# Feed-forward of an AdaLN block on one Trainium2 core: the gate-up groups of a step in one piece, the down products behind them

## The chip, the cores and the metric

One NeuronCore of a Trainium2 chip runs the whole program. The metric is the time of one execution on the device in microseconds (us), the median of three runs. TensorE (PE, with its weight loads as PEld), VectorE (DVE), ScalarE (ACT) and GpSimd (POOL) each work through their own list of instructions in order and wait for each other through semaphores. TensorE's matmul products go to eight PSUM banks of 128 x 512 float32; ScalarE and VectorE read them from there.

## The reference, cut to what matters

```python
h = _layernorm(x) * (1 + ca) + sa            # x is [1, 4096, 512]
x = x + ga * attn(h)                         # mixer: qkv, cumulative sums, SwiGLU
h = _layernorm(x) * (1 + cb) + sb
# feed-forward; weights are 4-bit values with a scale for each 128 inputs
gate_up = einsum('bsh,oh->bso', h, w_gu)     # 512 -> 2 * 1408
gate, up = gate_up[..., :1408], gate_up[..., 1408:]
hid = silu(gate) * up
y = einsum('bsi,hi->bsh', hid, w_down)       # 1408 -> 512
y = y / sqrt(mean(y * y) + 1e-6)
return x + gb * y
```

## The kernel before, in words

The program has two stages one behind the other: `mixer` (until about 1357 us of the span) and `ffn` (from there on). The change touches `ffn` alone.

`ffn` takes the 4096 tokens in NB = 8 blocks of T = 512. In a block it goes through I_T = 11 steps j, one for each 128 of the 1408 hidden units. A step has GROUPS = 8 gate-up groups m: m = 0 to 3 are the gate, one group for each 128 of the 512 inputs (they have scales of their own, so they can't be summed in PSUM), and m = 4 to 7 are the up part. A group is two matmuls (line 1856: the high and the low half of the activations) into one of the evacuation banks. Banks 0 to 3 serve in turn (`ev_bank`: m % 4). Bank 3 is also R, which takes the column sums for the norm, so in some steps (`r_steps`: step 5 of each block, steps 4 to 7 of block 0) the groups turn over banks 0 to 2 alone.

The groups are taken out of PSUM in pairs. ScalarE takes an even group (`take`, line 1926: copy with scale), then VectorE takes the odd one and adds the even (`take`, line 2119: multiply, add). GpSimd adds the two pair sums of the gate and of the up part (`half`, line 2008). ScalarE applies silu (line 1936), VectorE multiplies the two (`hidden`, line 2126), ScalarE rounds to the float16 part HH high (`high`, line 1932), GpSimd subtracts for the low part (`low`, line 2025). Each of these is one step late in its engine's order: behind the group-3 take of step j stands `hidden(j - 1)` on VectorE, ahead of the group-6 take `high(j - 1)` on ScalarE, and GpSimd does, in a step, half 0 of j, `low(j - 1)`, then half 1 of j.

The down product of a step is 4 output chunks c with 3 matmuls each (`down`, line 1820: high weights by high HH, low by high, high by low), 12 in all, summed over the 11 steps in banks 4 to 7. TensorE does it two steps late: in step j it does `down(b, j - 2, c)`. Only c = 0 waits for HH (both parts). For the first step of a block each c also waits for that chunk's bank to be copied out (`copy_y`, line 1894).

`before(j, m, steps)` gives the group that used a bank last; TensorE waits until that one is taken out before it starts group m.

Beside this, the previous block is finished at fixed places (place = 4 * j + m // 2, four in a step): ScalarE copies y out at places 8 to 11 (step 2), squares it at 12, 13, 14, 16 (line 1888); GpSimd adds the squares at 15, 16, 19 (line 2016); TensorE sums over partitions at 22 (`y_square`, line 1806, step 5, before m = 4), ScalarE keeps the sum (line 1908) and takes the root at 23 (line 1912, with an activation table load ahead of it and ahead of the next silu); VectorE takes groups 4 and 6 of that step in ScalarE's place (`open_tile`, line 2110), inverts at 24, 26, 27, 28 (line 2075) and multiplies, `norm_y` (line 2094), at 29, 32, 33, 36, each ahead of the odd take of its place; GpSimd adds the residual (`result`, line 2021) at 31, 35, 39, 43. Block 0 has, instead of this, the layer norm of the mixer's last block (lines 2065 to 2099 on VectorE, 1882 to 1916 on ScalarE, 1995 to 2003 on GpSimd).

A tile `A[slot]` of the taken groups and `HH[slot]` have two slots that alternate (the last step of a block has a third): the first take of step j waits for `low(j - 2)` (`slot_free`).

Of the kernel before, what the change touches and what calls it, by code (L numbers as in the profile page):

```python
# [1606 lines left out]
def ffn(nc, v):  # L1607


    T, NB, DT, I_T, GU, D = v["T"], v["NB"], v["DT"], v["I_T"], v["GU"], v["D"]  # L1610
# [4 lines left out]
    with ExitStack() as ctx:  # L1615
# [27 lines left out]
        def slot(j):  # L1643


            return 2 if j == I_T - 1 else j % 2
# [4 lines left out]
        def r_steps(b):  # L1651

            return range(4, 8) if first(b) else range(5, 6)

        def ev_bank(j, m, steps):
            return (GROUPS * (j - steps.start) + m + 1) % 3 if j in steps else m % 4

        def before(j, m, steps):

            for back, last in ((0, m), (1, GROUPS)):  # L1660
                same = [k for k in range(last) if ev_bank((j - back) % I_T, k, steps) == ev_bank(j, m, steps)]
                if same:
                    return back, same[-1]
            assert ev_bank(j, m, steps) == 3
            return None
# [25 lines left out]
        def first(b):  # L1691
            return isinstance(b, int) and b == 0
# [26 lines left out]
        def opened(b, j, m):  # L1719

            if by_vector(b, j, m):
                return opened_dve, len(OPENS) * b + opens(b).index((j, m)) + 1
            skipped = sum(1 for o in opens(b) if o < (j, m))
            return by_act, (DT * I_T - len(OPENS)) * b + DT * j + m // 2 + 1 - skipped
# [62 lines left out]
        @block.tensor  # L1787
        def _(pe):
            def sums_left(b, steps):

                pe.wait_ge(by_dve, DT * (I_T * b + steps.start))
                pe.wait_ge(*opened(b, steps.start - 1, GROUPS - 2))

            def mean():
                pe.wait_ge(x_sum, NSUM)
                nc.tensor.matmul(R[:], ones[:], RS[:], start=True, stop=True).then_inc(mean_red, 1)

            def variance():
                pe.wait_ge(sq_sum, NSUM)
                pe.wait_ge(centred, DT)  # L1800
                nc.tensor.matmul(R[:], ones[:], RS[:], start=True, stop=True).then_inc(var_red, 1)

            def y_square(b):
                pe.wait_ge(y_sum, NSUM * (b + 1))
                pe.wait_ge(*((var_kept, 1) if first(b) else (y_kept, b)))
                nc.tensor.matmul(R[:], ones[:], RSY[:], start=True, stop=True).then_inc(y_red, 1)

            def down(b, j, c):
                if c == 0:
                    if j == 0 and first(b):  # L1810
                        pe.wait_ge(down_loaded, 32)
                    pe.wait_ge(HH_high, I_T * b + j + 1)
                    pe.wait_ge(HH_low, I_T * b + j + 1)
                if j == 0 and first(b):
                    pe.wait_ge(last_ready, c + 1)
                elif j == 0:
                    pe.wait_ge(y_copied, DT * (b - 1) + c + 1)
                col = j * D + c * P
                for w, part in ((down_hi, 0), (down_lo, 0), (down_hi, 1)):
                    mm = nc.tensor.matmul(O[c][:], w[:, col:col + P], HH[:, slot(j), part, :],  # L1820
                                          start=(j == 0 and w is down_hi and part == 0),
                                          stop=(j == I_T - 1 and part == 1))
                if c == DT - 1:
                    mm.then_inc(down_used, 1)

            for b in range(NB):
                s, steps = b % 2, r_steps(b)
                if not first(b):
                    pe.wait_ge(H_loaded[s], 16 * ((b + 1) // 2))
                for j in range(I_T):  # L1830
                    for m in range(GROUPS):
                        place = DT * j + m // 2
                        if m % 2 == 0 and first(b) and place == MEAN:
                            sums_left(b, steps)
                            mean()
                        if m % 2 == 0 and first(b) and place == VARIANCE:
                            variance()
                        if m % 2 == 0 and not first(b) and place == Y_MEAN:
                            sums_left(b, steps)
                            y_square(b - 1)  # L1840
                        last = before(j, m, steps)
                        if last is None:
                            pe.wait_ge(*((var_kept, 1) if first(b) else (y_kept, b)))
                        elif not (j == 0 and last[0] and first(b)):

                            back, k = last
                            if k % 2:
                                pe.wait_ge(by_dve, DT * (I_T * b + j - back) + k // 2 + 1)
                            elif j < back:
                                pe.wait_ge(*opened(b - 1, I_T - 1, k))  # L1850
                            else:
                                pe.wait_ge(*opened(b, j - back, k))
                        which, g = m // DT, m % DT
                        col = (g * 2 * I_T + which * I_T + j) * P
                        for part in range(2):
                            mm = nc.tensor.matmul(EV[ev_bank(j, m, steps)][:], values[:, col:col + P], H[s][:, part, g, :],  # L1856
                                                  start=part == 0, stop=part == 1)
                        mm.then_inc(group_done, 1)


                        if m % 2:
                            if j >= 2:
                                down(b, j - 2, m // 2)
                            elif not first(b):
                                down(b - 1, I_T - 2 + j, m // 2)

            for j in (I_T - 2, I_T - 1):
                for c in range(DT):
                    down(NB - 1, j, c)
            pe.wait_ge(y_kept, NB - 1)  # L1870
            pe.wait_ge(by_dve, DT * I_T * NB)
            pe.wait_ge(*opened(NB - 1, I_T - 1, GROUPS - 2))
            for c in range(DT):
                pe.wait_ge(y_squared, DT * (NB - 1) + c + 1)
                mm = nc.tensor.matmul(R[:], ones[:], SQY[:, c, :], start=c == 0, stop=c == DT - 1)
            mm.then_inc(y_red, 1)
# [324 lines left out]
```

## Time and profile before

| what | before |
|---|---|
| median of 3 runs (lowest, highest) | 1942.83 us (1942.53, 1943.8) |
| the profiled execution: its time, its span | 1943.23 us, 1941.4 us |
| mean granted TensorE clock | 0.992 |
| TensorE busy over the span (matmul) | 1872.4 us, 96% |
| VectorE, ScalarE, GpSimd busy | 72%, 48%, 47% |
| stage `ffn` in the span | from 1356.95 us to the end |

The profile is of one execution. In a timeline row the first number is the start in us from the start of the span, the second the time until the last instruction of the row ended; neighbours of one kind are merged (x4), and matmul records overlap: a row of one matmul lasts 0.38 us while the next starts 0.2155 us after it. What stands in square brackets is the idle time of that engine ahead of the row, and who ended it.

### The profile page before, as it was taken

The page shows a single profiled execution, that of the slowest core. Times are in us where ns is not written, and L with a number is a line of the kernel's source. Part 1 is how long each engine was busy: PE and PEld are TensorE (multiplying, and loading weights), DVE is VectorE, ACT ScalarE, POOL GpSimd, SP SyncE. Part 2 cuts the span into 40 slices and gives each one's busy share as a digit, 9 for nine tenths or more (in the row PEclk, how much of TensorE's full clock was granted, in tenths as well). Part 3 has the DMA queues.
Part 4 walks back from the last instruction along what each step waited for, and adds up shares of the span by engine and source line. Part 5 has one row for each costly group of instructions (what it writes and reads, how often), then busy time and mean ns, then how long its engine had stood idle before and what let it go on. Part 6 is the DMA issues. An engine that isn't in the chain of part 4 may idle for free. (4 is left out here: it accounts for less than half of the span.)

```text
span 1941.4 us, 24528 instructions
## 1 busy us (share of the span) xinstructions
PE 1872.4 (96%) x8382; PEld 830.3 (43%) x8382; DVE 1399.3 (72%) x1787; ACT 924.8 (48%) x1414; POOL 909.7 (47%) x644
## 2 busy tenths in 40 slices
PE   6999999999999999999999999999999999999996
PEld 2443444444444444444444444444344444444442
DVE  6979768776867876877786686653677667767765
ACT  6753444235234434423533431221676766776673
POOL 2655435234314423422342331311768787777774
PEclk9999999999999999999999999999999999999998
DMA  8312220220202112021020121213210111011011
GB/s 309 130 55 65 76 70 24 75 66 18 81 20 70 51 40 69 11 87 60 24 74 17 48 66 33 88 39 113 118 44 22 44 66 59 8 66 66 1 44 65
DMA packets 70894, 120.44 MB, mean 62 GB/s; under 512 B 5024, under 2 KB 32672, under 8 KB 69152
## 3 DMA queue, kind: packets, MB, share of 16 engines
q1 hardware_dynamic: 70816, 119.45, 18.4%
q8 instruction: 43, 0.70, 0.1%
q14 instruction: 35, 0.29, 0.0%
HBM read 80.11 MB, written 39.32 MB: 62 GB/s over the span
## 5 line engine op out<-in xcount | busy, mean ns | idle before, releaser
L733 PE MATMUL bank<-Y,wsw 128*128 128x512 f16 x3072 | 689.9, 381 | 21.2 <-ACT late L939 14.4
L1140 POOL TENSOR_TENSOR late<-late 128x512 f16<-128x512 f32 x128 | 182.7, 1428 | 622.6 <-ACT late L947 621.9
L733 PEld LDWEIGHTS bank<-Y,wsw 128*128 128x128 f16 x3072 | 299.5, 98 | 394.6 <-ACT late L939 17.8
L2119 DVE SCALAR_TENSOR_TENSOR f_A<-bank,gu_s,f_A 128x512 f32<-128x512 f32 x352 | 259.9, 742 | 163.7 <-ACT f_A L1926 156.9
L708 PE MATMUL bank<-late,wout 128*128 128x512 f16 x1536 | 352.4, 379 | 0.4 <-POOL late L1140 0.4
L2008 POOL TENSOR_TENSOR f_A<-f_A 128x512 f32<-128x512 f32 x176 | 261.6, 1488 | 126.1 <-DVE f_A L2119 126.1
L1926 ACT ACTIVATE f_A<-bank,gu_s 128x512 f32<-128x512 f32 x336 | 229.1, 684 | 140.5 <-PE bank L1856 121.1
L1820 PE MATMUL bank<-f_HH,f_down_hi 128*128 128x512 f16 x704 | 266.8, 381 | 11.5 <-POOL f_HH L2025 11.2
L1206 DVE TENSOR_TENSOR late<-late,bank 128x512 f32<-128x512 f32 x128 | 87.3, 682 | 201.8 <-PE bank L733 192.7
L708 PEld LDWEIGHTS bank<-late,wout 128*128 128x128 f16 x1536 | 150.2, 98 | 188.8 <-issue 12.7
L939 ACT ACTIVATE late<-bank 128x512 f32<-128x512 f32 x128 | 76.4, 597 | 323.0 <-PE bank L733 279.4
L655 PE MATMUL bank<-H,wqkv 128*128 128x512 f16 x1008 | 225.8, 382 | 4.2 <-ACT H L800 4.2
L947 ACT ACTIVATE late<-late 128x512 f16<-128x512 f32 x128 | 80.4, 628 | 265.2 <-DVE late L1206 265.2
L1856 PE MATMUL bank<-H,wqkv 128*128 128x512 f16 x704 | 181.6, 379 | 2.9 <-DVE f_A L2119 1.9
L1856 PE MATMUL bank<-f_H,wqkv 128*128 128x512 f16 x704 | 182.2, 379 | 1.8 <-DVE f_A L2119 1.2
L655 PEld LDWEIGHTS bank<-H,wqkv 128*128 128x128 f16 x1008 | 99.1, 98 | 132.6 <-issue 20.4
L1820 PE MATMUL bank<-f_HH,f_down_lo 128*128 128x512 f16 x352 | 134.1, 381 | 0.0
L1820 PEld LDWEIGHTS bank<-f_HH,f_down_hi 128*128 128x128 f16 x704 | 69.0, 98 | 110.8 <-issue 34.5
L2025 POOL TENSOR_TENSOR f_HH<-f_A,f_HH 128x512 f16<-128x512 f32 x88 | 102.6, 1166 | 10.7 <-ACT f_HH L1932 10.6
L1322 DVE RECIPROCAL K<-K 128x512 f32<-128x512 f32 x32 | 107.0, 3344 | 0.0
L1856 PEld LDWEIGHTS bank<-H,wqkv 128*128 128x128 bf16 x704 | 67.3, 98 | 91.7 <-DVE f_A L2119 10.2
L1856 PEld LDWEIGHTS bank<-f_H,wqkv 128*128 128x128 bf16 x704 | 68.0, 98 | 88.7 <-DVE f_A L2119 6.6
(220 smaller groups left out, 2146.2 us busy)
## 6 DMA issues: line engine op xcount, KB each, us to landing
X<-xT SPq DMA_DIRECT2D x14, 1024.0 KB, 5.4
room<-packed SPq DMA_DIRECT2D x48, 176.0 KB, 2.4
h_scratch<-X SPq DMA_DIRECT2D x8, 1024.0 KB, 4.4
f_X<-x_scratch SPq DMA_DIRECT2D x8, 1024.0 KB, 5.5
x_scratch<-X SPq DMA_DIRECT2D x28, 256.0 KB, 2.2
h_scratch<-SQ SPq DMA_DIRECT2D x28, 256.0 KB, 2.2
outT<-f_X SPq DMA_DIRECT2D x7, 1024.0 KB, 4.3
room<-wswT SPq DMA_DIRECT2D x4, 1024.0 KB, 6.5
```

What stands on the lines that cost most here:

```text
L655: mm = nc.tensor.matmul(out[:], wqkv[:, pw, k, col:col + P], halves[:, px, k, :], start=(k == 0 and pw == 0 and px == 0), stop=(k == DT - ...
L708: mm = nc.tensor.matmul(O_BANK[c][:], wout[:, pw, j, c * P:(c + 1) * P], UG[:, j % 2, px, :], start=(j == 0 and pw == 0 and px == 0), stop ...
L733: mm = nc.tensor.matmul(out[:], wsw[:, pw, k, col:col + P], Y[:, px, k, :], start=(k == 0 and pw == 0 and px == 0), stop=(k == DT - 1 and ...
L1140: nc.gpsimd.tensor_tensor(UG[:, j % 2, 1, :], G, UG[:, j % 2, 0, :], ALU.subtract).then_inc(UG_low, 1)
L1206: nc.vector.tensor_tensor(dst, a, b_, ALU.mult).then_inc(done, 1)
L1322: nc.vector.reciprocal(K[:, c, :], K[:, c, :]).then_inc(inverted, 1)
L1820: mm = nc.tensor.matmul(O[c][:], w[:, col:col + P], HH[:, slot(j), part, :], start=(j == 0 and w is down_hi and part == 0), stop=(j == I_T ...
L1856: mm = nc.tensor.matmul(EV[ev_bank(j, m, steps)][:], values[:, col:col + P], H[s][:, part, g, :], start=part == 0, stop=part == 1)
L1926: nc.scalar.activation(A[:, slot(j), 2 * which + g // 2, :], EV[ev_bank(j, m, steps)][:], ACT.Copy, scale=gu_s[:, t, g:g + 1]).then_inc(by ...
L2008: nc.gpsimd.tensor_tensor(a, a, A[:, slot(j), 2 * which + 1, :], ALU.add).then_inc(halves, 1)
L2025: nc.gpsimd.tensor_tensor(HH[:, slot(j), 1, :], A[:, slot(j), 0, :], HH[:, slot(j), 0, :], ALU.subtract).then_inc(HH_low, 1)
L2119: nc.vector.scalar_tensor_tensor(a, EV[ev_bank(j, m, steps)][:], gu_s[:, which * I_T + j, g:g + 1], a, ALU.mult, ALU.add).then_inc(by_dve, 1)
```

## The change

In a step TensorE issued two groups, then the three down matmuls of chunk 0, two groups, chunk 1, and so on. Now it issues all eight groups, then the twelve down matmuls, chunk 0 to 3. Nothing else is changed: neither the instructions, nor their banks, nor the order on any other engine. The column sum of step 5 (and those of block 0 in steps 4 and 7) keeps its place between the groups.

```diff
                         mm.then_inc(group_done, 1)
 
-                        if m % 2:
-                            if j >= 2:
-                                down(b, j - 2, m // 2)
-                            elif not first(b):
-                                down(b - 1, I_T - 2 + j, m // 2)
+
+                    for c in range(DT):
+                        if j >= 2:
+                            down(b, j - 2, c)
+                        elif not first(b):
+                            down(b - 1, I_T - 2 + j, c)
 
             for j in (I_T - 2, I_T - 1):
                 for c in range(DT):
```

## Rows read from the trace of the kernel before

**Rows 1.** Windows: length, busy PE, PEld, DVE, ACT, POOL, clock, DMA, GB/s.

```profile
1357.00:1431.00 74.00, 66.70 (x294) 27.47 (x295) 54.87 (x76) 48.80 (x76) 50.67 (x37) 1.00 0.24 91
...
1602.90:1672.20 69.30, 68.38 (x312) 29.99 (x311) 48.33 (x66) 48.20 (x76) 53.84 (x41) 1.00 0.13 46
...
1920.00:1925.00 5.00, 4.32 (x12) 1.54 (x12) 0.00 (x0) 0.00 (x0) 0.54 (x1) 0.66 0.66 211
```

**Rows 2.** Timeline of TensorE: an ordinary step, the sum, two waits.

```profile
1602.88 1.03 PE L1856 MATMUL bank<-f_H,wqkv 128*128 128x512 f16 x4
...
1646.83 1.03 PE L1856 MATMUL bank<-H,wqkv 128*128 128x512 f16 x4
...
1648.34 1.03 PE L1856 MATMUL bank<-H,wqkv 128*128 128x512 f16 x4
...
1671.32 1.02 PE L1806 MATMUL bank<-f_RSY,ones 128*128 128x512 f32 x2
...
1672.17 0.59 PE L1856 MATMUL bank<-H,wqkv 128*128 128x512 f16 x2
...
1693.92 1.20 PE L1856 MATMUL bank<-H,wqkv 128*128 128x512 f16 x4
1695.84 0.38 PE L1820 MATMUL bank<-f_HH,f_down_hi 128*128 128x512 f16 x1 [0.72 <-POOL f_HH L2025]
```

**Rows 3.** Waits (total us, times, longest): 1602.9 to 1672.2; 1357 to 1431.

```profile
DVE f_A L2119 <- ACT f_A L1926: 19.3, 29, 1.4
...
ACT f_A L1926 <- POOL f_HH L2025: 5.5, 5, 1.5
```

**Rows 4.** Timeline of the first groups of block 0, without down products.

```profile
1356.95 5.50 PE L1856 MATMUL bank<-H,wqkv 128*128 128x512 f16 x24 [0.33 <-PEq L107]
...
1357.58 0.69 ACT L1926 ACTIVATE f_A<-bank,gu_s 128x512 f32<-128x512 f32 x1 [5.08 <-PE bank L1856]
...
1358.37 2.48 DVE L2119 SCALAR_TENSOR_TENSOR f_A<-bank,gu_s,f_A 128x512 f32<-128x512 f32 x3 [5.88 <-ACT f_A L1926]
...
1359.17 0.55 PEld L1856 LDWEIGHTS bank<-H,wqkv 128*128 128x128 bf16 x4 [0.40 <-DVE f_A L2119]
...
1360.04 0.55 PEld L1856 LDWEIGHTS bank<-H,wqkv 128*128 128x128 bf16 x4 [0.32 <-DVE f_A L2119]
```

**Rows 5.** Timeline of ScalarE in step 2 of block 4.

```profile
1650.08 0.59 ACT L1894 ACTIVATE f_Y<-bank 128x512 f32<-128x512 f32 x1
1650.56 0.69 ACT L1926 ACTIVATE f_A<-bank,gu_s 128x512 f32<-128x512 f32 x1
1651.13 0.61 ACT L1894 ACTIVATE f_Y<-bank 128x512 f32<-128x512 f32 x1
```

**Rows 6.** Timeline of VectorE, block 4: two `norm_y`, a take, `hidden`.

```profile
1684.36 0.74 DVE L2094 SCALAR_TENSOR_TENSOR f_Y<-f_Y,mod,f_RY 128x512 f32<-128x512 f32 x1
1685.01 0.74 DVE L2119 SCALAR_TENSOR_TENSOR f_A<-bank,gu_s,f_A 128x512 f32<-128x512 f32 x1
1685.68 0.68 DVE L2126 TENSOR_TENSOR f_A<-f_A 128x512 f32<-128x512 f32 x1
...
1695.81 1.66 DVE L2094 SCALAR_TENSOR_TENSOR f_Y<-f_Y,mod,f_RY 128x512 f32<-128x512 f32 x1
```

**Rows 7.** Timeline of GpSimd, block 4, steps 7 to 9.

```profile
1685.84 1.65 POOL L2008 TENSOR_TENSOR f_A<-f_A 128x512 f32<-128x512 f32 x1 [1.48 <-DVE f_A L2119]
1687.45 1.15 POOL L2025 TENSOR_TENSOR f_HH<-f_A,f_HH 128x512 f16<-128x512 f32 x1
1688.57 1.72 POOL L2021 TENSOR_TENSOR f_X<-f_X,f_Y 128x512 f32<-128x512 f32 x1
...
1695.65 1.27 POOL L2021 TENSOR_TENSOR f_X<-f_X,f_Y 128x512 f32<-128x512 f32 x1
```

**Rows 8.** Timeline of the end of the last block's chain, two engines.

```profile
1917.96 0.69 DVE L2126 TENSOR_TENSOR f_A<-f_A 128x512 f32<-128x512 f32 x1 [2.38 <-POOL f_A L2008]
...
1920.68 0.50 PE L1820 MATMUL bank<-f_HH,f_down_hi 128*128 128x512 f16 x1 [2.39 <-POOL f_HH L2025]
```

## The prediction

> **What bounds it now.** I read the windows first, then TensorE's timeline, then the waits. In a whole block of the feed-forward TensorE is busy 68.38 of 69.30 us at granted clock 1.00, while VectorE, ScalarE and GpSimd are at 48 to 54 us [rows 1]: TensorE sets the pace, and only what makes it wait can cost or bring time. An ordinary step repeats each quarter in 1.51 us [rows 2]: seven matmuls of 0.2155 us, four of the groups and three of the down product, so no wait at all. From sum to sum a block takes 1672.17 - 1602.88 = 69.29 us [rows 2]. Its 308 matmuls need 308 x 0.2155 = 66.37 us, and the float32 sum 0.86 us (1671.32 to 1672.17 [rows 2], rounded up), together 67.23. So **2.05 us of a block are waits**. Followed row by row, 1.35 of them stand ahead of chunk 0 of the down product, where HH is late: 1.05 in step 9 (it should have followed at 1693.92 + 0.86 = 1694.78, it came at 1695.84 [rows 2]; 0.17 of that may be a bank, its four-row lasts 1.20 instead of 1.03), the rest 0.13 and 0.17. About 0.6 are waits for a bank (steps 2, 5, 6).
>
> **What changes.** The matmuls, their number and time stay. No instruction, DMA or semaphore is added, and only TensorE's order moves. Two terms follow.
>
> *Removed: the waits for HH.* The low part of step j - 2 is ready in step j - 1 (reckoned below: 5.9 us after its start), and chunk 0 now comes 3.5 us into step j instead of 0.86. With 2.6 us more slack, 1.35 us a block go.
>
> *Added: waits for banks.* Two groups were followed by 0.65 us of down product; now eight run behind each other with four banks. I take a step's start as 0; a group lasts 0.431. ScalarE's take starts 0.63 after the group's start (1357.58 - 1356.95), VectorE's 0.79 after ScalarE's (1358.37), and lasts 0.75 (0.74 at 1685.01); TensorE starts again 0.05 after that [rows 4, 6]. So group 1 is out at 0.63 + 0.79 + 0.75 = 2.17, group 5 starts at 2.22 instead of 5 x 0.431 = 2.155: +0.07. Group 2 is taken at 1.49, group 3 at 2.28, out at 3.03; group 7 starts at 3.08 as it would anyway. The trace holds this very pattern, twelve groups without a down product: the weight loads wait until 1359.17 (2.22 after the start) and 1360.04 (3.09), and 24 matmuls take 5.50 us against 23 x 0.2155 + 0.38 = 5.34 [rows 4]. Hence **0.07 in an ordinary step** (0, 1, 4, 9, 10).
>
> In the other steps something stands ahead of a take that TensorE waits for. Before, the down matmuls covered it.
> - Step 2. The first copy waits for the last down matmul, starts at 0.22; copy to take is 0.48, take to copy 0.57 [rows 5]. Takes at 0.70 and 1.75: group 1 out at 2.24, group 3 at 3.29, so groups 5 and 7 start at 2.30 and 3.34: 0.33.
> - Step 3, squares for copies: the first lies ahead of the step, group 7 alone is late: 0.29.
> - Step 5, three banks: group 3 waits for group 0 (+0.08); group 7 waits for group 4, which VectorE takes behind `hidden` (2.28, 0.67 to `hidden`, whose 0.68 [rows 6] hold the next for about 0.6: 3.55, out at 4.30, start at 4.35, against 3.96): 0.47.
> - Step 6: roots and table loads end late, the first take comes at 0.79 rather than 0.63: 0.23.
> - Step 7: a `norm_y` at 2.09 ahead of the group-3 take, 0.65 from start to next start [rows 6]: that take at 2.74, group 7 at 3.53: 0.51 with the 0.07.
> - Step 8: the same, but GpSimd is in the way. Its chain after step 7's group-3 take (out at 3.48) is half, low, result, half: 1.65 + 1.15 + 1.72 [rows 7] + 1.27, less overlaps, until 9.24, which is 2.69 of step 8. A `norm_y` that meets a GpSimd addition lasts 1.66 instead of 0.74: it began at 1695.81 while `result` ran until 1696.92, and ended 0.55 behind it [rows 6, 7]. So here it ends at 3.24, the take at 3.91, group 7 at 3.96: 0.94.
>
> Sum: 5 x 0.07 + 0.33 + 0.29 + 0.47 + 0.23 + 0.51 + 0.94 = 3.12 us. Against 2.05: **+1.07 us a block, x 7 = +7.5**. Bounds: both norms free gives +0.2 a block; the norms meeting GpSimd in full each time (+0.9 for step 7) gives +2.0.
>
> By the Trainium skill (SBUF — State Buffer, "Who interferes with whom") a VectorE instruction with two SBUF inputs is held until a running GpSimd instruction is done; that is what these rows show. Without such a rule step 8 would cost 0.51, and the sum would be 3 us less.
>
> **HH still in time?** The group-3 take is out at 3.03, `hidden` from 2.95 to 3.62, `high` 3.66 to 4.29, half 0 until 4.7, `low` until 5.9. The first take of the next step (6.11 + 0.63) needs that: 0.8 us to spare.
>
> *Block 0* has waits for 9.9 us now (72.8 us from its first group to the second block's, 62.9 of matmuls). HH's 3.5 or so go; waits of the first takes for `low` (5.5 us in all [rows 3]) mostly go. But four steps have three banks: group 3 +0.08, group 4 waits for group 1 (2.22 against 1.80), group 7 for group 4 (+0.21), 0.71 a step; and its subtractions, inverses and multiplies stand ahead of group-1 and group-3 takes. My walk gives 11.4: **+1.5**, between -2 and +4.
>
> *The end.* Step 10 to the last down: the last odd take comes at 5.77 instead of 5.95, but GpSimd's chain (low, result, half) reaches 8.25 against 8.97. Then `hidden`, `high`, `low` follow as from 1917.96 to 1920.68 [rows 8]: **-0.7**. TensorE waits about as long, so the clock falls there as now (0.66 [rows 1]).
>
> Total: 7.5 + 1.5 - 0.7 = +8.3 on the profiled 1943.23 us, 1951.5; the median lies 0.4 lower: **1951.1 us**.
>
> **Rivals.**
> 1. *Faster: the removed wait decides.* HH's 1.35 a block are seen, the new bank waits are reckoned. From bank waits under 1.4 us a block on, the kernel is faster by over 0.2%. With 1.0 (each extra slides behind the takes that matter) it is 7 x -1.05, -0.7 and -1.5 for block 0: 1933. Against it: in 19.3 us of a block VectorE's take waits for ScalarE [rows 3], the pair is a chain that has no slack with four banks. 10%.
> 2. *No change.* Both norms find a gap (steps 7 and 8 at 0.07): 7 x -0.24 + 0.8 gives 1942; with half of it, 1945. 19%.
> 3. *GpSimd becomes late.* In steps 3, 4, 7, 8 it has 5.8 us and more of work in a step of 6.1 to 7. If `low` ends past the next step's first take, as in block 0 (up to 1.5 us [rows 3]), each block loses 1 us more: 1958. 13%.
> 4. *The clock falls.* Behind the 2.39 us wait near the end the mean clock was 0.66 [rows 1, 8]; twelve down matmuls (2.59 us) take 1.3 us more at that. Once a block is 9 us more: 1960. Against it: block 4's 1.05 us wait left the clock at 1.00, and the new waits are shorter than 1 us. The Trainium skill (TensorE: Matmul & The Clock Gate, "A second HAM failure mode: psum-queue depth-cycling") tells of kernels in which short pauses between groups, as the banks turn, made the clock swing between its two levels; no row of block 1 to 7 shows it before the end. 3%.
>
> **How the numbers follow.** My case has 55%, 1947 to 1956. What this kernel's measurement can tell from no change is 0.2%, 3.9 us. Slower by that: 55 + 13 + 3 and a little of the border of case 2, 72%; within it 18%; faster 10%. The range leaves out case 1, most of case 4: 1943 to 1959.
>
> **What the changed profile would show.** Right: no TensorE wait on line 1820 for HH in blocks 1 to 7 but for the end; the weight load of group 5 waiting for VectorE's take in each step, 2.2 us after its start; a block of about 70.4 us, steps 2, 3, 5, 7, 8 the long ones; GpSimd and ScalarE busy as before; a `norm_y` of 1.2 us or more in step 8. Wrong: a block under 69 us, group 7 on time in steps 7 and 8, or `low` as the last releaser of a first take.

## The result, and the profile after

| what | before | after |
|---|---|---|
| median (lowest to highest, runs) | 1943.16 us (1942.53 to 1943.8, 6) | 1949.01 us (1948.57 to 1953.51, 6) |
| ratio to before, 95% interval | | 1.0035 [1.0022, 1.0048] |
| profiled execution: time, span | 1943.23, 1941.4 us | 1949.07, 1947.3 us |
| one block, from column sum to column sum | 69.29 us | 70.58 us (twice of six 70.93) |

The kernel became slower by 0.35% by the ratio, which compares means; the medians are 5.85 us apart. The interval lies clear of 1, so the loss is beyond the noise. The forecast was 1951.1.

The windows of the kernel after: one block; one of the two that are 0.35 us longer; the first block; the end. The columns are those of [rows 1].

```profile
1603.70:1674.30 70.60, 69.29 (x312) 28.79 (x311) 46.47 (x66) 48.20 (x76) 53.57 (x40) 1.00 0.12 46
1674.30:1745.20 70.90, 69.33 (x311) 28.84 (x310) 46.33 (x66) 48.18 (x76) 53.53 (x40) 1.00 0.12 45
1356.00:1430.00 74.00, 68.82 (x296) 26.62 (x297) 55.08 (x77) 48.80 (x77) 50.84 (x38) 1.00 0.25 96
...
1925.00:1931.00 6.00, 3.67 (x17) 1.30 (x14) 0.69 (x1) 0.64 (x2) 1.52 (x2) 1.00 0.68 226
```

Busy time says little here: TensorE's "busy" even rose (69.29 against 68.38), because a short pause vanishes in the overlap of matmul records. Starts say it. TensorE's timeline after, block 4: the sum and step 5, then steps 7 and 8, then step 9 (answers to [rows 2]).

```profile
1673.43 1.02 PE L1806 MATMUL bank<-f_RSY,ones 128*128 128x512 f32 x2
1674.29 1.46 PE L1856 MATMUL bank<-H,wqkv 128*128 128x512 f16 x6
1675.96 0.61 PE L1856 MATMUL bank<-H,wqkv 128*128 128x512 f16 x2 [0.22 <-DVE f_A L2111]
...
1685.27 3.27 PE L1856 MATMUL bank<-H,wqkv 128*128 128x512 f16 x14
1688.82 0.60 PE L1856 MATMUL bank<-H,wqkv 128*128 128x512 f16 x2 [0.28 <-DVE f_A L2120]
...
1691.85 3.27 PE L1856 MATMUL bank<-H,wqkv 128*128 128x512 f16 x14
1695.79 0.39 PE L1856 MATMUL bank<-H,wqkv 128*128 128x512 f16 x1 [0.66 <-DVE f_A L2120]
...
1698.82 3.70 PE L1856 MATMUL bank<-H,wqkv 128*128 128x512 f16 x16
1702.35 0.38 PE L1820 MATMUL bank<-f_HH,f_down_hi 128*128 128x512 f16 x1
```

Fourteen matmuls take 14 x 0.2155 = 3.02 us from start to next start. In step 7 group 7 should follow at 1688.29 and comes at 1688.82, 0.53 late; in step 8 at 1694.87, and it comes at 1695.79, 0.92 late. In step 9 sixteen matmuls take 3.53 instead of 3.45: 0.08, the ordinary step. There is no wait ahead of line 1820 left in the block; [rows 2] had 1.05 us in step 9, of which 0.17 stood ahead of its group 1, for a bank, and 0.88 ahead of the down product.

The ordinary step close up (step 9), as in [rows 4]:

```profile
1699.45 0.69 ACT L1927 ACTIVATE f_A<-bank,gu_s 128x512 f32<-128x512 f32 x1 [1.33 <-PE bank L1856]
1700.24 1.61 DVE L2120 SCALAR_TENSOR_TENSOR f_A<-bank,gu_s,f_A 128x512 f32<-128x512 f32 x2 [1.11 <-ACT f_A L1927]
...
1701.04 0.55 PEld L1856 LDWEIGHTS bank<-H,wqkv 128*128 128x128 bf16 x4 [0.40 <-DVE f_A L2120]
...
1701.90 0.12 PEld L1856 LDWEIGHTS bank<-H,wqkv 128*128 128x128 bf16 x2 [0.32 <-DVE f_A L2120]
```

The step starts at 1698.82; the take of group 0 at +0.63, VectorE's at +1.42, and the weight load of group 5 waits for it until +2.22, that of group 7 until +3.08.

VectorE and GpSimd in steps 7 and 8 of the same block: the two `norm_y` ahead of group-3 takes, and `result` with the late half (answers to [rows 6] and [rows 7]).

```profile
1687.36 0.74 DVE L2095 SCALAR_TENSOR_TENSOR f_Y<-f_Y,mod,f_RY 128x512 f32<-128x512 f32 x1
1688.02 0.74 DVE L2120 SCALAR_TENSOR_TENSOR f_A<-bank,gu_s,f_A 128x512 f32<-128x512 f32 x1
...
1693.95 1.12 DVE L2095 SCALAR_TENSOR_TENSOR f_Y<-f_Y,mod,f_RY 128x512 f32<-128x512 f32 x1
1694.99 0.74 DVE L2120 SCALAR_TENSOR_TENSOR f_A<-bank,gu_s,f_A 128x512 f32<-128x512 f32 x1
```

```profile
1691.58 1.71 POOL L2022 TENSOR_TENSOR f_X<-f_X,f_Y 128x512 f32<-128x512 f32 x1
1693.25 1.27 POOL L2009 TENSOR_TENSOR f_A<-f_A 128x512 f32<-128x512 f32 x1
```

The second `norm_y` starts while GpSimd's half runs until 1694.52, and ends 0.55 behind it, at 1695.07: 1.12 instead of 0.74.

GpSimd's work behind that differs from before. In the kernel before, the late half of step 7 and the first half of step 8 ran in a row; `hidden` waited for the one and was held up by the other; and `low` of step 7, which makes HH complete, ended at 1695.70, 8.0 us after the start of step 8. Its rows of GpSimd, then of VectorE:

```profile
1690.24 3.00 POOL L2008 TENSOR_TENSOR f_A<-f_A 128x512 f32<-128x512 f32 x2
1694.54 1.16 POOL L2025 TENSOR_TENSOR f_HH<-f_A,f_HH 128x512 f16<-128x512 f32 x1 [1.29 <-ACT f_HH L1932]
```

```profile
1692.12 1.67 DVE L2126 TENSOR_TENSOR f_A<-f_A 128x512 f32<-128x512 f32 x1 [0.56 <-POOL f_A L2008]
```

In the changed kernel GpSimd has 1.29 us to spare ahead of the first half of step 8, and the same `low` ends at 1698.58, 6.7 us after the start of the step:

```profile
1695.81 1.65 POOL L2009 TENSOR_TENSOR f_A<-f_A 128x512 f32<-128x512 f32 x1 [1.29 <-DVE f_A L2120]
1697.42 1.16 POOL L2026 TENSOR_TENSOR f_HH<-f_A,f_HH 128x512 f16<-128x512 f32 x1
```

The waits of one block after (1603.7 to 1674.3; total, times, longest), to [rows 3]:

```profile
DVE f_A L2120 <- ACT f_A L1927: 21.4, 21, 1.8
...
PEld bank L1856 <- DVE f_A L2120: 9.2, 21, 1.2
```

The same row of before had 1.1 us in two waits; 21 times in a block TensorE's weight loads now stand behind VectorE's take.

### The profile page after: what moved, and what is told of

Its sections match the earlier page's. It is cut to its first block and busy times, and to the rows that moved or that the text cites. A ratio compares the mean times of both kernels' runs of the same rounds, so it can differ in the third digit from the quotient of the medians.

```text
span 1947.3 us, 24528 instructions
## 1 busy us (share of the span) xinstructions
PE 1876.9 (96%) x8382; PEld 819.7 (42%) x8382; DVE 1386.0 (71%) x1787; ACT 924.7 (47%) x1414; POOL 907.9 (47%) x644
## 5 line engine op out<-in xcount | busy, mean ns | idle before, releaser
L655 PE MATMUL bank<-H,wqkv 128*128 128x512 f16 x1008 | 224.9, 381 | 3.8 <-ACT H L800 3.8
L1820 PE MATMUL bank<-f_HH,f_down_hi 128*128 128x512 f16 x704 | 223.6, 379 | 2.3 <-POOL f_HH L2026 2.3
L1856 PE MATMUL bank<-H,wqkv 128*128 128x512 f16 x704 | 169.5, 380 | 9.6 <-DVE f_A L2120 7.6
L1856 PE MATMUL bank<-f_H,wqkv 128*128 128x512 f16 x704 | 167.7, 380 | 5.5 <-DVE f_A L2120 4.1
L1856 PEld LDWEIGHTS bank<-H,wqkv 128*128 128x128 bf16 x704 | 61.1, 98 | 112.4 <-DVE f_A L2120 43.4
L1856 PEld LDWEIGHTS bank<-f_H,wqkv 128*128 128x128 bf16 x704 | 62.1, 98 | 104.6 <-DVE f_A L2120 37.1
```

The source lines that it names most:

```text
L655: mm = nc.tensor.matmul(out[:], wqkv[:, pw, k, col:col + P], halves[:, px, k, :], start=(k == 0 and pw == 0 and px == 0), stop=(k == DT - ...
```

## The experiments

Each was timed beside the kernel before on the same chip, 5 to 12 times. "Block" is the time from one column sum to the next in the profile, the usual one of the six; where "twice" or two numbers stand, single blocks of that profile differ. The waits of single steps are gaps between the starts of TensorE's matmuls, in block 4. A total can differ by 1 to 2 us for reasons that the change has no part in (see "The end" below), so small differences are read from the blocks.

### Four groups at a time

```diff
-                        if m % 2:
+                        for c in {3: (0, 1), 7: (2, 3)}.get(m, ()):
                             if j >= 2:
-                                down(b, j - 2, m // 2)
+                                down(b, j - 2, c)
```

(not shown: the branch for the first two steps of a block changes in the same way)

> TensorE issues four gate-up groups, then down chunks 0 and 1, four groups, then chunks 2 and 3; all else as before. Theory (the eight-group piece is slower because its groups 5 and 7 wait for evacuation, while the waits for HH it removes are worth 1.35 us a block): four groups need no more than the four banks, so the bank waits of the big piece do not arise, and chunk 0 comes 1.72 us into the step instead of 0.86, so 0.86 us of each HH wait goes: 0.13, 0.17 and all but 0.2 of the 1.05 in step 9. A block of about 68.2 us instead of 69.29, total 1943.2 - 7 - 1 or 2 in block 0 = 1934 to 1937. Rival (any order in which the down products do not follow each pair is slower, since takes come in bursts): 1944 or more.

Measured: 1941.24 us, ratio 0.9995 [0.9986, 1.0004], a block of 69.17 us. No change against before; against the eight at once, 1.4 us a block less. The rival falls: an order in which the down products do not follow each pair need not be slower; it is the eight groups in a row that cost. But the expected gain did not come either. In step 9, where before had waited for HH, TensorE now waits for a bank:

```profile
1692.16 1.83 PE L1856 MATMUL bank<-H,wqkv 128*128 128x512 f16 x6
1694.23 0.61 PE L1856 MATMUL bank<-H,wqkv 128*128 128x512 f16 x2 [0.25 <-DVE f_A L2119]
```

Six matmuls need 1.29 us; it takes 2.07, so 0.78 of the 1.05 is there again, under another name. The waits of fours for banks in steps 5 to 7 are 0.9 us together, as much as those of before in all steps but the ninth.

### The new order in step 9 alone

```diff
-                        if m % 2:
+                        for c in (range(DT) if m == GROUPS - 1 else ()) if j == 9 else ((m // 2,) if m % 2 else ()):
```

(not shown: `down` below it takes c instead of m // 2)

> The kernel before, but with the changed order (eight groups, then twelve down products) in step 9 of each block alone. Theory: the HH wait of step 9 (1.05 us) goes, the ordinary 0.08 us for group 5 comes: a block of 68.3 us, total 1943.2 - 7 x 0.97 = 1936.4, block 0 about the same or 0.5 less. Rival (the lateness behind the wait, the GpSimd chain, is only handed on to step 10): the wait shows up in step 10 and the total is 1941 or more.

Measured: 1948.48 us, 1.0036 [1.0023, 1.0049], a block of 70.37 us. The expectation was wrong by 2 us a block, with the wrong sign. The total lies where its rival had it (1941 or more), but the wait was not handed on to step 10: it stands in step 9 itself. Step 9 of block 4:

```profile
1695.26 1.78 PE L1856 MATMUL bank<-H,wqkv 128*128 128x512 f16 x6
1697.29 1.19 PE L1856 MATMUL bank<-H,wqkv 128*128 128x512 f16 x4 [0.25 <-DVE f_A L2119]
1699.54 1.47 PE L1856 MATMUL bank<-H,wqkv 128*128 128x512 f16 x6 [1.05 <-DVE f_A L2119]
```

TensorE waits 0.74 and 1.39 us for VectorE's takes. What happens there on VectorE and GpSimd:

```profile
1693.47 1.67 DVE L2126 TENSOR_TENSOR f_A<-f_A 128x512 f32<-128x512 f32 x1 [0.56 <-POOL f_A L2008]
...
1697.15 1.67 DVE L2094 SCALAR_TENSOR_TENSOR f_Y<-f_Y,mod,f_RY 128x512 f32<-128x512 f32 x1
1698.74 1.40 DVE L2119 SCALAR_TENSOR_TENSOR f_A<-bank,gu_s,f_A 128x512 f32<-128x512 f32 x2
```

```profile
1691.57 3.02 POOL L2008 TENSOR_TENSOR f_A<-f_A 128x512 f32<-128x512 f32 x2
...
1697.00 1.27 POOL L2021 TENSOR_TENSOR f_X<-f_X,f_Y 128x512 f32<-128x512 f32 x1
```

`hidden` waits for a half that GpSimd has late (two halves in a row, 3.02 us, behind `result`), and then lasts 1.67 instead of 0.68; the last `norm_y` meets `result` and lasts 1.67 instead of 0.74. Both hold up VectorE's takes. So the wait for HH in step 9 of the kernel before is the end of a backlog of GpSimd and VectorE. Giving HH 2.6 us more removes the wait for HH (it is complete 3.8 us before TensorE asks for it), but not the time: VectorE's takes are as late, and eight groups in a row need them.

### The new order in steps 2, 3, 5, 7 and 8 alone

The same line with `j in (2, 3, 5, 7, 8)`.

> The kernel before, but with the changed order in steps 2, 3, 5, 7 and 8 alone, those with work of the other engines ahead of a take. Theory: their bank waits (0.35 + 0.32 + 0.49 + 0.53 + 0.91 = 2.60 us) come, of before 0.1 + 0.22 + 0.13 + 0.17 = 0.62 go, and the HH wait of step 9 stays at about 1 us or less: a block of 69.29 + 1.98 = 71.3 us, total 1943.2 + 7 x 1.98 = 1957 (block 0 within 3 us). If the lengthened steps 7 and 8 give GpSimd the time to catch up, step 9's wait shrinks by up to 1 us: 1950. Rival (the loss of the change sits in the ordinary steps): 1943 to 1946.

Measured: 1948.82 us, 1.0034 [1.0021, 1.0047], a block of 70.41 us: the second of the two numbers expected (1950). That is all but 0.17 of the 1.29 us a block that the change costs. The five steps do not cost the same one by one, though: step 7 waits 0.88 us here and 0.53 in the changed kernel, and the five together 2.96 against 2.5. Step 9 has no wait any more: with steps 7 and 8 longer, GpSimd catches up. It stands idle for 1.29 us ahead of the first half of step 8, and `low` of step 7 ends 6.7 us after the start of step 8, both as in the rows of the changed kernel above. That is how the lateness behind the HH wait went in that kernel too.

### The norm multiplications moved: later, then first in their steps

```diff
-        NORM_Y = {29: 0, 32: 1, 33: 2, 36: 3}
+        NORM_Y = {30: 0, 32: 1, 34: 2, 36: 3}
+        NORM_Y = {28: 0, 32: 1, 36: 2, 40: 3}
```

The first new line was run on the changed kernel.

> The changed kernel, with the multiplications norm_y 0 and 2 on VectorE one place later (places 30 and 34 instead of 29 and 33), behind the group-3 take and hidden instead of ahead of the group-3 take. Theory: the waits of TensorE for group 7 in steps 7 and 8 (0.45 and 0.83 us) go, leaving 0.08 a step, 1.28 us x 7 = 9 us: 1949 - 9 = 1940, a block of 69.3 us. Rival (GpSimd chain or another late take holds these steps anyway): the waits move to another group or to the next step, 1946 to 1949.

Measured: 1945.47 us, 1.0022 [1.0013, 1.003], a block of 70.04 (twice 70.38). Step 7 fell to 0.09 as expected, but step 8 kept 0.54 and step 9 got 0.35: behind `hidden` and ahead of group 1 a `norm_y` met GpSimd each time (1.55 to 1.77 us each). The block gained 0.54 of the 1.28 us expected and the total 3.5 of 9: the rival's mechanism, the waits moving to another group and the next step, took the rest.

The second new line was run on the changed kernel, on fours and on the kernel before, in this order.

> The changed kernel, with the four norm_y on VectorE at places 28, 32, 36 and 40, the first of their steps: behind the last take of the step before, none ahead of a group-3 take; result stays on GpSimd at 31, 35, 39, 43. Theory: the waits for group 7 in steps 7 and 8 (0.53 and 0.92 us) fall to the 0.09 of an ordinary step, with at most 0.2 more in step 7, whose first take now stands behind an inversion and a norm_y: a block of 69.4 instead of 70.6 us, total about 1941. Rival (any norm_y costs TensorE its time in this order, wherever it stands): 1945 to 1949.

Measured: 1946.08 us, 1.0022 [1.0013, 1.0031], a block of 69.90 (twice 70.26). TensorE in steps 7, 8 and 9:

```profile
1684.75 1.89 PE L1856 MATMUL bank<-H,wqkv 128*128 128x512 f16 x8
1687.15 1.47 PE L1856 MATMUL bank<-H,wqkv 128*128 128x512 f16 x6 [0.51 <-DVE f_A L2120]
...
1691.04 3.70 PE L1856 MATMUL bank<-H,wqkv 128*128 128x512 f16 x16
...
1697.17 3.70 PE L1856 MATMUL bank<-H,wqkv 128*128 128x512 f16 x16
```

Steps 8 and 9 are ordinary (3.70 for sixteen, as step 9 above): the 0.92 us of step 8 was the `norm_y` ahead of the group-3 take. Step 7 waits 0.68, more than the 0.3 allowed: the multiplication needs the last inversion's end, and then stands ahead of the take of group 1. So the total, 1946.08, came out where the rival had it (1945 to 1949): of the four multiplications the first still costs TensorE its time, the other three do not.

> The order of four groups and two chunks, with norm_y at 28, 32, 36, 40. Theory: what is left of waits in steps 8 and 9 of that order (0.9 us) came from two norm_y that meet GpSimd within two steps; with one a step half of it or more goes: a block of 68.3 to 68.7 instead of 69.17 us, total 1935 to 1938. Rival: GpSimd's backlog with result is there anyway, 1940 or above.

Measured: 1943.94 us, 1.0007 [0.9998, 1.0016], a block of 69.57 us: 0.4 more than fours with the old places. The total is the rival's (1940 or above), and 1.6 us over the 1942.37 of before. Three waits of 0.34 to 0.39 us for banks stand in one block, none of them large. I did not follow them further.

> The kernel before, with norm_y at 28, 32, 36, 40. Theory: the HH wait of step 9 (1.05 us) has the same root and shrinks to 0.3 or less: a block of 68.5 us, total about 1937 to 1938. Rival: it stays, 1942.

Measured: 1939.42 us, 0.9984 [0.9975, 0.9993], a block of 68.70 us. The wait for HH in step 9 is gone, with TensorE's order of before and `result` where it was, so its cause was the place of the multiplications. The total is 1.4 us above what was expected, for the same 0.5 us in step 7.

### The residual additions on VectorE

```diff
-        RESULT = {31: 0, 35: 1, 39: 2, 43: 3}
+        RESULT = {31: 0, 34: 1, 35: 2, 38: 3}
```

(not shown: the call of `result` goes from GpSimd's `beside` to VectorE's.) On the changed kernel, on that with norms at 30 and 34, on before, and on fours:

> The changed kernel, with the four residual additions (result) done by VectorE at places 31, 34, 35 and 38 instead of by GpSimd at 31, 35, 39 and 43. Theory (in step 8 the norm_y ahead of the group-3 take is held up by GpSimd, whose second half of step 7 is late behind result): without result GpSimd is through by then, the wait of TensorE for group 7 in step 8 falls from 0.92 to the 0.53 of step 7, the latter stays: a block of 70.2 instead of 70.6 us, total about 1946. Rival A (norm_y alone makes step 8's wait): block unchanged, 1949. Rival B (the additions now hold up takes on VectorE): over 1949.

> As the run before, and norm_y 0 and 2 one place later (30 and 34) as in the run with the moved norms. Theory: the moved norms alone left waits of 0.54 and 0.35 us for group 5 in steps 8 and 9, because norm_y 1 and 3 were held up by result on GpSimd; without it steps 7, 8 and 9 wait 0.1 each: a block of 69.3 us, total about 1940, faster than before by 2 to 3 us. Rival (VectorE is too full in steps 7 to 9 once it has the additions too): waits stay at 0.5 and more in step 8, 1944 or above.

> The kernel before, with the additions on VectorE. Theory (the 1.05 us wait for HH in step 9 of each block is the backlog of GpSimd with result in steps 7 and 8, whatever the order of TensorE): it goes, a block of 68.2 instead of 69.3 us, total about 1935. Rival (it is a question of how soon after the step's start chunk 0 comes): the wait stays above 0.5 us, 1940 or above.

> The order of four groups, two chunks, four groups, two chunks, with the additions on VectorE. Theory: the wait of 0.8 us in step 9 that was left in the order of fours goes, and no HH wait can come: a block of 68.2 us, total about 1934, level with the order of pairs or 1 to 2 us under it. Rival (pairs and fours differ in more than HH): over 1937.

| kernel | total, us | ratio to before | block, us |
|---|---|---|---|
| changed + additions on VectorE | 1949.23 | 1.0036 [1.0023, 1.0050] | 70.76 |
| the same, norms at 30 and 34 | 1954.79 | 1.0066 [1.0053, 1.0080] | 71.47 |
| before + additions on VectorE | 1941.38 | 0.9996 [0.9987, 1.0005] | 69.33 to 69.70 |
| fours + additions on VectorE | 1942.66 | 1.0003 [0.9994, 1.0012] | 69.69 |

In the first the wait in step 8 fell from 0.92 to 0.53, exactly step 7's, as expected: without `result` GpSimd is through when that `norm_y` comes. But additions ahead of takes made a new wait of 0.63 in step 9, 0.45 of it for group 5, and the total stayed, as its rival B had it (over 1949). In all four the additions (two SBUF inputs, 0.68 us alone) lasted up to 1.77 us beside GpSimd. The totals of the last three came out where their rivals had them. For the second the rival's reason shows too: waits of 0.63 in step 8 and 1.68 in step 9, VectorE's order is too full. In the third the wait for HH left step 9 and came in step 8 (0.62 us), with 0.25 and 0.38 for banks in steps 9 and 10; in the fourth step 9 waits 1.39 us for banks. So the expectation that `result` on GpSimd alone makes the wait of step 9 was not borne out: taking it away put as much waiting elsewhere.

### One norm multiplication a step, in the order of before

```diff
-        NORM_Y = {29: 0, 32: 1, 33: 2, 36: 3}
+        NORM_Y = {29: 0, 32: 1, 36: 2, 40: 3}
```

> The kernel before (pairs and chunks in turn), with norm_y at 29, 32, 36 and 40. Theory: with norm_y 0 at place 28 TensorE waited 0.5 us in step 7, since that multiplication stood right behind the last inversion and held the first take; one place later it is hidden as in the kernel before, the rest stays as in the run with 28: a block of 68.3 to 68.4 instead of 68.7 us, total about 1937, faster than before by 0.25 to 0.3%. Rival (norm_y 0 and 1 in steps 7 and 8 then meet result again): the wait for HH in step 9 comes back in part, 1939 to 1942.

Measured: 1935.38 us, 0.9965 [0.9953, 0.9978], a block of 68.24 us: the fastest kernel here, 6 us under the 1941.39 of before beside it. The expectation held, the rival did not. Its waits in one block (1667 to 1735.2) have no row for HH on line 1820 left; TensorE's only named ones are short:

```profile
PEld bank L1856 <- DVE f_A L2119: 0.6, 1, 0.6
...
PEld bank L1856 <- ACT f_A L1926: 0.2, 1, 0.2
```

Its matmuls need 67.23 us a block; 1.0 us of waits is left: 0.31 for a bank in step 6, and 0.1 to 0.2 each ahead of chunk 0 in steps 2, 5, 7 and 8, where HH is complete just before it is used (in step 2 HH has been there for 0.5 us, and it is y's copy).

## Why the prediction was right, and where its steps were not

**Waits for banks: right.** Read from the profile after, against the text: ordinary step 0.08 (0.07 foretold), step 2 0.35 (0.33), step 3 0.32 (0.29), step 5 0.10 + 0.39 (0.47), step 6 0.23 (0.23), step 7 0.53 (0.51), step 8 0.92 (0.94). They sum to 3.2 us against 3.12, and the block came to 70.58 against 70.36. The ground for it was a stretch of the old trace with the pattern of the new order [rows 4]. That these waits are the cost is shown by fours (1.4 us a block less with half the length of the piece), by the five steps alone (most of the loss, with steps 2, 3 and 8 waiting as in the changed kernel), and for step 8 by the multiplications put first. One sign asked for was missed: a `norm_y` of 1.2 us or more in step 8. It lasted 1.12, and the prediction's own times (from 2.09 to 3.24 in the step) had said 1.15. The other signs of being right came, and none of being wrong.

**Waits for HH: the size was right in the changed kernel, the mechanism was not.** The step was "With 2.6 us more slack, 1.35 us a block go". They are gone in the profile after. But in step 9 alone the same slack brought no time: 1.05 us for HH and a bank became 2.1 us for banks. The 1.05 us was a backlog of GpSimd and VectorE behind two `norm_y` and `result` in one step; the changed kernel clears it since steps 7 and 8 last longer. The prediction counted step 9 among the ordinary ones (0.07) and gave no reason why VectorE's takes should be on time there. They were, by what steps 7 and 8 lose: that part was luck. The two effects are hence not two terms to be added step by step, and none of the orders tried (eight, four, eight in step 9 or in five steps alone) had rival 1's gain, HH without the banks. Of the 1.35 us the prediction also had the parts a little wrong: 0.17 of step 9 is a bank's, and the 0.2 us ahead of chunk 0 in step 5, which it took for a bank's, is HH (`low` ends 0.15 us before the matmul starts, as in steps 7 and 8). The sum is the same. With one multiplication a step the wait of step 9 is gone in TensorE's old order (68.24, 68.70 us).

With the multiplications at 28, 32, 36, 40, a block lasts 68.70 in the order of before and 69.90 in the new one, 1.20 apart; at the old places 69.29 and 70.58, 1.29 apart. The price of the new order is nearly the same in both.

**GpSimd's hold on VectorE: right,** with the times foretold: the `norm_y` in step 8 ended 0.55 behind the half, and without `result` that step fell to step 7's 0.53. In the changed profile, from 1460 to 1905 us, 25 VectorE instructions with two SBUF inputs (19 `norm_y`, 6 `hidden`) started while GpSimd was adding, and all 25 ended 0.55 us behind it; the 194 takes that did so (one input from PSUM) lasted 0.65 to 0.75 us like the rest. The rule of the Trainium skill (SBUF — State Buffer, "Who interferes with whom"), that a VectorE instruction with two SBUF inputs is blocked by a GpSimd instruction that has started, agrees with every such pair here.

**Block 0: mis-sized.** Foretold +1.5 us, it came to about -0.5. From the first group to block 1's sum it is 106.39 us before and 105.28 after; at that sum 6 down matmuls (1.29 us) are still outstanding that before had done, and 0.7 us of the difference belongs to block 1. So 105.28 + 1.29 - 0.7 - 106.39 = -0.5. The prediction's 72.8 us is a little misread: from first group to first group it is 71.4, and the next 1.4 us are a wait ahead of block 1's group 1, which the change took away. Its walk of the new order had 11.4 us of waits; about 9 came. It gives that sum alone, so which of its steps was too dear stays open.

**The end: right in the chain, wrong in the clock.** From the start of the last step to the last down product for which TensorE waits it is 11.16 us (1917.04 to 1928.20) against 11.80 before, -0.64 (foretold -0.7). But the clock did not fall there:

```profile
1928.20 0.38 PE L1820 MATMUL bank<-f_HH,f_down_hi 128*128 128x512 f16 x1 [2.28 <-POOL f_HH L2026]
...
1931.73 0.67 PE L1876 MATMUL bank<-f_SQY,ones 128*128 128x512 f32 x1 [0.78 <-ACT f_SQY L1985]
```

From the wait's end to the next sum 3.53 us at clock 1.00, where before took 5.22 (1920.68 to 1925.90) at 0.66 to 0.72: -1.7. This is not an effect of the change. In the profiles of the fourteen kernels run here, one each, the last wait for HH is 2.28 to 2.40 us in ten. Behind it the clock fell in six of them (before, fours, the five steps alone, the multiplications first on the changed kernel and on before, one a step), and stayed at 1.00 in four (the changed kernel, norms at 30 and 34, step 9 alone, fours with the multiplications first). The same order of TensorE stands on both sides, with the same wait (2.28 and 2.29 us for the changed one). What decides it stays open.

**The sum.** 7 x 1.29 = 9.0, two longer blocks 0.7, block 0 -0.5, the end -0.64 - 1.7, and the stage ahead, which nothing changed, was 0.9 shorter in this execution (1356.06): together +6.0 us; the spans differ by 5.9. Of this the clock and the stage ahead (-2.6 us together) are chance of this execution: the stage ahead, the same code everywhere, lasted from 1355.0 to 1357.6 us in the fourteen profiles. The rest, +8.6, stands against the forecast of +8.3. That these agree so well is in part luck: the seven blocks cost 9.7 us with the two longer ones, 2.2 more than foretold, and block 0 cost 2.0 less.

**The extra 0.35 us** of two blocks stays open. Each time it sits in one step (step 10 of block 2, step 0 of block 5), where a VectorE take starts 0.35 us later than its operands allow, and the profile names TensorE's matmul, done long before. Single blocks 0.35 us longer or shorter are in eight more of the profiles, some with TensorE's other orders. No run was made to test it.

Rival 2 (no change) was refuted by steps 7 and 8, rival 3 by the waits: no first take waits for `low` in the block after. Rival 4 did not come: the clock is 1.00 in all blocks, with waits of 0.07 to 0.9 us in every step.

## What to carry to other kernels

When work is put in longer pieces, count the buffers of the piece that has the turn: eight groups on four banks expose every instruction that stands ahead of a take, and its price can be added from the rows where the same pattern already runs. A wait of the pacing engine names the last releaser alone; before counting it as won, see whether the engines behind it are late as well, for then it can come back under another name. Here the better cure for that wait was to spread the side work of VectorE, one multiplication a step (0.35% faster), not to reorder TensorE.

## What the runs showed of the hardware that was not expected

- Near-equal waits of TensorE at the end of the kernel (2.28 to 2.40 us, ten profiles) were followed by a fall of the clock in six and by none in four: 4.85 to 5.22 us from the wait's end to the next sum, or 3.53.
- A `norm_y` on VectorE (two SBUF inputs) took from 0.74 to 1.83 us with the same operands, by whether GpSimd was adding at that moment; moving one multiplication by one place (from 28 to 29) moved the total by 3.7 us of 1940, by the two ratios to before.
- It works the other way too: in the changed profile a GpSimd addition that started while such a VectorE instruction ran took 1.64 to 1.73 us instead of 1.27, and one that was already running kept its 1.27.
- TensorE's busy time rose by 0.9 us a block while it waited 1.3 us more: pauses shorter than the overlap of two matmul records (0.17 us) do not show as idle.
